# Routing of a graph network's expert layer: second expert from shifted logits, fewer vector instructions, row factors kept in the row

## What is computed

```python
x = x + gnn(layernorm(x), edges)
f = layernorm(x)
rh = relu(f @ router_w1 + router_b1)
expert_logits = softmax(rh @ router_w2 + router_b2)     # 6 of them
top_w, top_i = top_k(expert_logits, 2)
routing_weights = softmax(top_w)                        # two weights a node
x = x + sum over the two experts of weight * expert(f)  # three matmuls an expert
```

## Time and profile before

| | us |
|---|---|
| median of three runs | 6377.77 (6375.88 to 6379.18) |
| profiled execution, time | 6376.87 |
| profiled execution, span from first to last instruction | 6375.1 |
| graph half, up to the routing stage | 5293 |
| routing stage | about 5293 to 5635 |
| tile tables and region tails | about 5634 to 5668 |
| tile stage | about 5668 to 6375 |

### The profile page before, as it was taken

The page is one execution under the profiler, slowest core; times in us unless marked ns, Lnnn a source line. Parts: engine busy times, 40 slices in busy tenths (PEclk is TensorE's granted clock), DMA queues, the critical chain, the costliest instruction groups (busy, mean ns, idle before and its releaser), DMA issues. The chain is left out here.

```text
span 6375.1 us, 79641 instructions
## 1 busy us (share of the span) xinstructions
PE 4356.3 (68%) x15178; PEld 2151.3 (34%) x15179; DVE 1894.7 (30%) x6972; ACT 1191.2 (19%) x2762; POOL 3431.6 (54%) x3661
## 2 busy tenths in 40 slices
PE   4566766666666767656666666667666665559999
PEld 4322222222222222232222222222222223448888
DVE  7311111212121111251112211211212216656665
ACT  5100000000000000120000000000000005535554
POOL 0466666666666666566666666666666661321111
PEclk5667676776766666766776667666776766679999
DMA  4633333333333333243333333333333332321111
GB/s 115 203 107 88 88 90 88 88 89 87 89 88 89 90 88 87 76 125 89 88 88 88 89 88 89 89 88 89 88 88 87 89 87 69 108 74 48 50 49 45
DMA packets 261857, 564.42 MB, mean 89 GB/s; under 512 B 67263, under 2 KB 136225, under 8 KB 261794
## 3 DMA queue, kind: packets, MB, share of 16 engines
q0 software_dynamic: 171264, 466.46, 25.3%
q1 hardware_dynamic: 90530, 97.27, 5.4%
HBM read 503.39 MB, written 60.09 MB: 88 GB/s over the span
## 5 line engine op out<-in xcount | busy, mean ns | idle before, releaser
L610 POOL DMA_INDIRECT ring<-messages,idx_stage x3328 | 3147.7, 946 | 1878.6 <-issue 875.7
L1612 PE MATMUL ps<-ring,onehot_mem 128*64 128x256 f32 x6656 | 2758.9, 539 | 1272.3 <-DMA ring<-messages,idx_stage 611.4
L1612 PEld LDWEIGHTS ps<-ring,onehot_mem 128*64 128x64 f32 x6656 | 952.1, 179 | 2731.9 <-DMA ring<-messages,idx_stage 1564.5
L1105 DVE TENSOR_TENSOR acc<-acc,ps 128x128 f32 x832 | 239.8, 288 | 3763.1 <-remote 1985.4
L744 ACT ACTIVATE win_rows<-ps 64x256 f32<-64x256 f32 x832 | 312.6, 377 | 2172.7 <-PE ps L1612 1120.9
L1094 DVE TENSOR_SCALAR onehot_mem<-iota_bf,tables 128x64 f32<-128x64 bf16 x3344 | 645.2, 266 | 232.4 <-issue 164.5
L1510 PE MATMUL ps<-ident,win_rows 64*128 64x64 f32 x1664 | 335.2, 293 | 404.8 <-ACT win_rows L744 319.6
L733 ACT ACTIVATE idx_stage<-tables 128x8 int32 (+1 forms) x420 | 87.1, 208 | 2371.5 <-PE ps L1612 1010.6
L1510 PEld LDWEIGHTS ps<-ident,win_rows 64*128 64x128 f32 x1664 | 204.8, 172 | 900.8 <-issue 900.8
L1817 PE MATMUL ps<-acc 128*128 128x256 f32 x2048 | 466.6, 380 | 0.8 <-ACT acc L907 0.8
L669 POOL DMA_INDIRECT out_dram<-acc x128 | 128.3, 1002 | 599.1 <-DVE acc L1463 415.4
(11 more groups left out here) (249 smaller groups left out, 2159.0 us busy)
## 6 DMA issues: line engine op xcount, KB each, us to landing
ring<-messages,idx_stage POOLq DMA_INDIRECT x3328
rows_mem<-in_x_dram SPq DMA_DIRECT2D x54, 448.0 KB, 4.2
acc<-routed_rows SPq DMA_DIRECT2D x64, 264.0 KB
messages<-dinvT SPq DMA_DIRECT2D x23, 448.0 KB, 6.2
dinvT<-in_x_dram SPq DMA_DIRECT2D x22, 448.0 KB, 4.0
messages<-ring SPq DMA_DIRECT2D x19, 448.0 KB, 3.2
dinvT<-dinv_row SPq DMA_DIRECT2D x28, 224.0 KB
messages<-rows_mem SPq DMA_DIRECT2D x14, 448.0 KB, 3.2
```

The costliest lines, as they stand in the source:

```text
L610: pool.indirect_dma_start(out=slots[:, s, :], out_offset=None, in_=t_dram[layer], in_offset=bass.IndirectOffsetOnAxis(ap=idx_stage[:, u, s ...
L1105: dve.tensor_tensor(sums(w, WIN), sums(w, WIN), ps[:, 2 + u, 0:KH * WIN].rearrange("p (k w) -> p k w", k=KH), ALU.add).then_inc(ev_fast, 1)
L1612: pe.matmul(ps[0:WIN, u, 0:D], onehot[:, u, j, 0:WIN], slots[:, s, :], start=j == 0, stop=j == CPG - 1).then_inc(chunks_used, 1)
```

## The change

- Of a row's eight extra words, two change their meaning: instead of mean and reciprocal root, `x*r + s` is kept as the factor `r` and the addend `s = -mean*r`, and `row_shift` writes both straight into the row. The two copies at the end of `xf_rows` go, and so do the copies of the best expert's mark and of the node number: the mark is computed in its place (X_BEST), and the number is kept in the row buffer and advanced there (four instructions ahead of the loop set it up).
- `row_vars` has six instructions instead of seven, and the first three of them don't wait for one another.
- The best and the second-best expert are found from the shifted logits (the best one is zero there) and no longer from the probabilities. `route1` grows from three to eight small instructions and is where the first exponential is released; that exponential takes a seventh column, the second-best logit, so that `gap` comes out of one instruction. A new `pair_of` (five instructions) ends in `mb_ready`; `route2` is three instructions, `route3` four.
- VectorE's order becomes: `x1_rows` twice, `row_vars`, `route4` of the pair before, `route1`, `row_shift`, `xf_rows`, `pair_of`, `route2`, `route3`, `places`.
- In the tile stage `norm_rows` multiplies and adds where it subtracted and multiplied.

```diff
 def row_vars(p):
-    mean_var(st8, sum8, dif8, m28, mean8, var8, var_steps.step).then_inc(var_done, 1)
+    dve.tensor_tensor(sum8, st8[:, :, 1], st8[:, :, 4], ALU.add)
+    dve.tensor_tensor(m28, st8[:, :, 2], st8[:, :, 5], ALU.add)
+    step(dve.tensor_tensor(dif8, st8[:, :, 1], st8[:, :, 4], ALU.subtract))
+    step(dve.scalar_tensor_tensor(out=dif8, in0=dif8, scalar=0.25, in1=dif8, op0=ALU.mult, op1=ALU.mult))
+    step(dve.scalar_tensor_tensor(out=var8, in0=m28, scalar=1.0 / D, in1=dif8, op0=ALU.mult, op1=ALU.add))
+    dve.tensor_scalar(var8, var8, EPS, None, ALU.add).then_inc(var_done, 1)
+def row_shift(p, q):
+    dve.wait_ge(sd_done, p + 1)
+    hold(dve)
+    var_steps.step(dve.reciprocal(xrow[q][:, :, X_RSTD], var8.unsqueeze(2)))
+    dve.scalar_tensor_tensor(out=xrow[q][:, :, X_SHIFT], in0=sum8.unsqueeze(2), scalar=-0.5, in1=xrow[q][:, :, X_RSTD],
+                             op0=ALU.mult, op1=ALU.mult).then_inc(rstd_ready, 1)
+    dve.wait_ge(rstd_ready, p + 1)
 def route1(i, q):
-    rstep(dve.tensor_reduce(flat(lmax), lg, AX.X, ALU.max))
-    dve.tensor_tensor(lg, lg, over(lmax), ALU.subtract).then_inc(sh_done, 1)
+    rstep(dve.tensor_reduce(flat(lmax), lgx, AX.X, ALU.max))
+    rstep(dve.tensor_tensor(lgx, lgx, over(lmax), ALU.subtract))
+    rstep(dve.scalar_tensor_tensor(out=cand, in0=lgx, scalar=0.0, in1=across(mark), op0=ALU.is_equal, op1=ALU.mult))
+    rstep(dve.tensor_reduce(first, cand, AX.X, ALU.min))
+    rstep(dve.tensor_tensor(m1st, across(mark), over(first), ALU.is_equal))
+    rstep(dve.scalar_tensor_tensor(out=rest, in0=m1st, scalar=-1e30, in1=lgx, op0=ALU.mult, op1=ALU.add))
+    dve.tensor_reduce(lg[:, :, NX:NX + 1], rest, AX.X, ALU.max).then_inc(sh_done, 1)
+def pair_of(i, q):
+    ...
+    rstep(dve.tensor_tensor(eq, rest, over(second), ALU.is_equal))
+    rstep(dve.tensor_tensor(cand, eq, across(mark), ALU.mult))
+    rstep(dve.tensor_reduce(flat(which2), cand, AX.X, ALU.min))
+    rstep(dve.tensor_tensor(duo, first, which2, ALU.add))
+    ...
+    dve.tensor_tensor(mb_bf, across(duo_mark), duo.to_broadcast([RB, B2, NDUO]), ALU.is_equal).then_inc(mb_ready, 1)
 def route2(i):
-    ...                                   # probabilities, best twice, duo, mb_bf: 16 instructions
+    rstep(dve.tensor_reduce(flat(lsum), ex[:, :, 0:NX], AX.X, ALU.add))
+    rstep(dve.reciprocal(lrec, lsum))
+    dve.scalar_tensor_tensor(out=gap, in0=ex[:, :, NX:NX + 1], scalar=-1.0, in1=lrec,
+                             op0=ALU.add, op1=ALU.mult).then_inc(gap_done, 1)
 def route(i, q, next1, next2):            # VectorE
     ...
     row_vars(i + 1)
+    if before:
+        route4(i - 1, (q - 1) % XBUFS)
-    route1(i)
-    if not isinstance(i, int) or i > 0 and late(i - 1):
-        route4(i - 1, (q - 1) % XBUFS)
+    route1(i, q)
+    row_shift(i + 1, (q + 1) % XBUFS)
     xf_rows(i + 1, (q + 1) % XBUFS)
+    pair_of(i, q)
     route2(i)
     route3(i, q)
     places(i)
```

More of the change, by code:

```diff
@@ L269, in gnn_moe @@
         XBUFS = len(xrow)
+        X_ID, X_FIRST, X_SECOND, X_BEST, X_SHIFT, X_RSTD = [slice(D + n, D + n + 1) for n in range(6)]
         zb = [old_ring.take(P, KH, CH), Region(onehot_mem).take(P, KH, CH)]
@@ L811, in norm_x, with row_sd @@
                 last.then_inc(xhat_done, 1)
+            def row_sd(p):
+                act.wait_ge(var_done, p + 1)
+                hold(act)
+                act.activation(var8, var8, ACT.Sqrt).then_inc(sd_done, 1)
             def norm_x1(p, q):
@@ L1253, in _ @@
             var_steps, xf_steps, route_steps = Chain(dve, var_chain), Chain(dve, xf_chain), Chain(dve, route_chain)
-            VAR_STEPS, ROUTE_STEPS, PLACE_STEPS = 6, 21, 2
+            VAR_STEPS, ROUTE_STEPS, PLACE_STEPS = 4, 17, 2
+            for q in range(XBUFS):
+                dve.tensor_scalar(xrow[q][:, :, X_ID], node_ids.unsqueeze(2), float((q - XBUFS) * 2 * CH), None, ALU.add)
             def x1_rows(t, u, par, p, q):
@@ L1312, in late, with route1 @@
                 return not isinstance(i, int) or i < PAIRS - 3
-            def route1(i):
-                route_steps.begin(i * ROUTE_STEPS - (PLACE_STEPS if not isinstance(i, int) or i > 0 and late(i - 1) else 0))
+            def route1(i, q):
+                first = xrow[q][:, :, X_BEST]
                 dve.wait_ge(lg_mm, i * 2 + 2)
                 logits = ps[0:RB, 7, 0:B2 * 8].rearrange("p (b n) -> p b n", b=B2)[:, :, 0:NX]
-                dve.tensor_tensor(lg, logits, across(rb2_sb), ALU.add).then_inc(lg_read, 1)
+                lgx = lg[:, :, 0:NX]
+                dve.tensor_tensor(lgx, logits, across(rb2_sb), ALU.add).then_inc(lg_read, 1)
@@ L1320, in route1 @@
                 dve.wait_ge(lg_read, i + 1)
-                rstep(dve.tensor_reduce(flat(lmax), lg, AX.X, ALU.max))
-                dve.tensor_tensor(lg, lg, over(lmax), ALU.subtract).then_inc(sh_done, 1)
-            def best(values, largest, where):
-                rstep(dve.tensor_reduce(flat(largest), values, AX.X, ALU.max))
-                rstep(dve.tensor_tensor(eq, values, over(largest), ALU.is_equal))
-                rstep(dve.tensor_tensor(cand, eq, across(mark), ALU.mult))
-                rstep(dve.tensor_reduce(flat(where), cand, AX.X, ALU.min))
+                hold(dve)
@@ L1370, in route @@
                 a, small = i * 2 + 2, not isinstance(i, int) or i >= 0
+                before = not isinstance(i, int) or i > 0 and late(i - 1)
+                if small:
+                    route_steps.begin(i * ROUTE_STEPS - PLACE_STEPS * before)
                 if next1:
@@ L1386, in route @@
                         route4(i, q)
-                    before = not isinstance(i, int) or i > 0 and late(i - 1)
                     assert route_steps.n == ROUTE_STEPS + PLACE_STEPS * (before - late(i))
```

57 lines of the change are left out of this document (22 added, 35 removed).

## The result

On the chip of the forecast's own measurement the kernel after takes 6357.15 us (median of nine runs, 6353.06 to 6363.53) and the kernel before 6373.86 us (nine runs, 6365.12 to 6379.18; its first three are the 6377.77 of the forecast). The ratio is 0.9975, 95% interval 0.9965 to 0.9985: 16 us faster, 10 to 22.

The account below looks back on a forecast made before the run. It took the routing stage to be bound by TensorE's completions held while scatters are issued. Ten periods at 1.01 us (10.1) plus 2.2 at the ends gave 12.3 us off: 6365.5 us, range 6360 to 6386.

Parts of the forecast that it names:

- The reading: Routing stage: TensorE's completions are held while scatters are issued; scatters starting 1.01 us sooner cut the period from 23.92 to 22.91.
- Items 1 and 2: VectorE ahead of the addresses: shorter row_vars gains 0.42 us, route4 ahead of route1 0.59; ten periods give 10.1 us.
- Items 3 to 6: Routing stage beside the scatters: later normalized rows, ranks and exponentials, shorter route2 and route3; all hidden, costing nothing.
- Ends of the stage: Routing stage's opening body and pairs 0, 11, 12 and 13, outside the ten held periods: sum -2.2 us.
- pair 11 at -1.0: Routing stage's tail: pair 11 follows a batch of scatters that starts 1.0 us sooner, so -1.0 us.
- pair 12 with its ranks and router matmuls "0.4 sooner": Routing stage's tail: mb_ready comes 1.2 us sooner, the turns 0.87 later, so ranks and router matmuls come 0.4 sooner.
- the tail's waits: Last pairs of the routing stage: waits of several us each, allowed for in the case's range of 6360 to 6371 us.
- The base: Whole kernel before: profiled execution 6376.87 us, the median of the runs 0.9 above it; the gain is taken off this.
- Rival A: Routing stage: the turned rows' word is held before L836, making periods 1.2 us longer; 6392.6 us, chance 0.12.
- Rival B: Routing stage: no word is held, TensorE itself is late and its ranks come 0.8 us later; 6383.6 us, chance 0.12.
- Rival C: Routing stage: release is tied to TensorE's clock, the period stays 23.9 us, only the ends change; 6375.6 us, chance 0.16.

Follow-up runs that it names:

- k2_split: Kernel after with each pair's eight scatters issued as four, then four once the next pair's ranks are read, first kind of chip: 6319.24 us, ratio 0.99 to before.
- m3_split6: Kernel after with six scatters issued, the other two once the next pair's ranks are read, first kind of chip: 6336.35 us, ratio 0.9922 to before.
- m1_before: Kernel before, unchanged, run again for a second trace on the first kind of chip: 6387.92 us, ratio 1.0008 to itself.
- k1_after: Kernel after, unchanged, run again on the first kind of chip: 6369.04 us, ratio 0.997 to the kernel before.
- m2_route4_back: Kernel after with route4 moved behind the whole of route1, first kind of chip: 6391.73 us, ratio 1.0014 to the kernel before.
- k4_warm_after: Kernel after with 22 idle matmuls more per pair on TensorE, first kind of chip: 6377.68 us, ratio 0.9987 to the kernel before.
- r1_before: Kernel before, unchanged, run for its trace on the second kind of chip: 5559.46 us.
- g2_warm_after: Kernel after with 22 idle matmuls more per pair on TensorE, second kind of chip: 5541.26 us, ratio 0.9951 to the kernel before.
- r1_after: Kernel after, unchanged, run for its trace on the second kind of chip: 5547.58 us.

## Why the prediction was wrong

- The reading (TensorE's word is held while scatters are issued): right on this kind of chip, shown by k2_split and m3_split6. On the other kind nothing was held, which the trace of before could not show.
- Items 1 and 2, the steady pairs: right. row_vars takes 0.86 us to L1384 (0.89), the scatters start at 11.27 (11.31), ten periods give 9.6 us (10.1); against the second trace of before (m1_before and k1_after) they give 7.6. The small steps without a wait start 0.08 to 0.09 apart. The rule of the Trainium skill (VectorE: DVE Perf Modes, The DRAIN you can't avoid) that leaving out the semaphores saves nothing does not fit them, or the period would be 23.1 and not 22.9; the section itself says that a next instruction that is not held starts earlier.
- Items 3 to 6, hidden: right. xf_rows starts at T+12.85 and ends at T+14.2 (14.2), the turned rows are kept at T+16.2 (16.2).
- Ends of the stage: the step that failed, pair 11 at -1.0 and pair 12 with its ranks and router matmuls "0.4 sooner". Measured were +1.5 and -6.2. The terms were built from VectorE's and TensorE's own times and took the held words of the earlier trace rows as given. They were not: they came with two batches in nearly one row, since the ranks of pair 11 were let through 0.12 us before a batch's last scatter. In after the read fell behind the batch and the next one began after a gap. The tail, pairs 11 to 13, gave 5.2 us instead of 2.4, and 6.1 in the second pair of traces (m1_before and k1_after); m2_route4_back shows the tail in one row again, at +8.9. Why the word comes early there is not shown: in before, m1_before and m2_route4_back the ranks of pair 11 ended 4.4 to 4.7 us into the batch and were let through early, in after and k1_after 6.2 to 6.3 us into it and were held; but in k4_warm_after they ended 4.4 us into it too and were held all the same. The prediction named the tail's waits as "several us each", but left only 5.5 us below the forecast for them and for the base together.
- The base: the median of three runs of before was 3.9 us above the median of nine. 12.3 us off the latter is 6361.6, in the range. So the miss of 8.4 us is 3.9 us of base and 2.8 us of tail; the rest, 1.7 us, is within what the first line of the table shows of the variation from run to run (5.7 us ahead of any changed instruction of the loops).
- Rival A: wrong for this change, L844 was prompt (0.29 us idle before it); right as a mechanism (k4_warm_after). Rival B: wrong, TensorE's ranks were 4.6 us old when they were read. The Trainium skill (SBUF — State Buffer, Who interferes with whom) says that TensorE waits for nobody and that a DMA doesn't contend with an engine; the trace agrees for the matmuls, whose turns of 0.93 us inside a batch (5591.70 in before) take the same on the second kind of chip, but the word of them came late. Rival C: wrong here, since the period moved. On the second kind of chip, a case that the prediction didn't have, the long pairs of before are those whose turns are slow (1.3 to 1.7 us; granted clock 0.50 in the one shown above).

What stays open: why the hold exists on one kind of chip and not on the other; which words it catches; and what the change gains by on the second kind beyond the clock, where the kernel after itself ran only once. The hold is not simply "until the batch ends": the ranks of pair 11 in before ended at 5590.26 and were read at 5594.20, with the batch still running, and an early pair of m2_route4_back went free.

## What to carry to other kernels

When two engines that wait for different work resume at the same moment, look for what else ended then, and test it by moving that alone: four scatters ahead of the wait instead of eight gave three times what the whole change gave. A wait of several us that is not inherent but comes from how two bursts happen to fall is not a constant of the forecast; ask at each such wait if the change moves the bursts apart, and let the range take in its full length on both sides. A trace from one chip tells what bounds the kernel on that chip: here the change gained 0.25 and 0.3% on the first kind, and two kernels that contain it 0.3% on the second, where the start of the scatters, which sets the period on the first, made no difference.

## What the runs showed of the hardware

The two kinds of chip differ long before the routing stage. In the graph half, where GpSimd issues 3328 gathers, VectorE's L1105 waits for TensorE; the group's row in the first trace of before, then in r1_before:

```profile
L1105 DVE TENSOR_TENSOR acc<-acc,ps 128x128 f32 x832 | 239.8, 288 | 3763.1 <-remote 1985.4
```

```profile
L1105 DVE TENSOR_TENSOR acc<-acc,ps 128x128 f32 x832 | 240.1, 289 | 3139.8 <-PE ps L1510 3138.5
```

The gathers themselves take the same time (946 and 948 ns each). On the first kind more than half of the wait ends with no instruction that fits the time, as before L1358. Of the 817 us between the spans of these two traces 766 lie ahead of the first ranks' read, and this wait differs by 623. That it is the same hold is argued from these rows, not shown.

Idle matmuls that had TensorE at 2.4 GHz for the turns (granted clock 1.00 instead of 0.51) were worth 8 us in ten pairs of the kernel after where words come at once (g2_warm_after against r1_after), and cost 9 us where they are held (k4_warm_after), as another word fell into the hold.
